# A vision-tower layer on one Trainium2 core: table stage, relu in PSUM and the last tree, changed together

## The reference

```python
dA = (1.0 + dtA / 2) / (1.0 - dtA / 2)
V = jnp.exp(log_dA[:, :, None] * jnp.arange(L))
K = 2.0 * jnp.einsum('chn,hnl->chl', C_term, V).real
```

```python
for level in range(DEPTH):
    n = 2 ** level
    g = gate[:, n - 1:2 * n - 1]
    f = jnp.stack([1.0 - g, g], axis=-1)
    lp = lp * broadcast(f).reshape(BT, M)
```

## Time and profile before

| what | value |
|---|---|
| times shown | 501.42, 502.08, 502.32 us |
| profiled execution, its own time | 502.32 us |
| its span, first to last instruction | 500.5 us |
| what lies around the span | 1.82 us |
| mean granted TensorE clock | 0.989 of full |
| busy: PE, DVE, ACT, POOL | 442.5, 353.1, 293.3, 193.0 us |
| chain that ended last, share by engine | PE 67%, DVE 14%, issue 6%, POOL 5%, ACT 3%, DMA 2% |

### The profile page before, as it was taken

How to read it: one execution, slowest core, us unless ns; L and a number is a source line. 1 busy time by engine, 2 the same in 40 slices (tenths; PEclk the granted TensorE clock), 3 DMA queues, 4 the chain that set the end, 5 groups by cost and what they waited for, 6 DMA issues and landing times.

```text
span 500.5 us, 11532 instructions
## 1 busy us (share of the span) xinstructions
PE 442.5 (88%) x3897; PEld 404.0 (81%) x3897; DVE 353.1 (71%) x837; ACT 293.3 (59%) x612; POOL 193.0 (39%) x185
## 2 busy tenths in 40 slices
PE   0099668899999999999999999999999999998993
PEld 0069667787888898988988988988988988988992
DVE  5999987997877785546486486486486486485685
ACT  3824654788876777467357357356356356356641
POOL 0495997642442110516306306306306306305102
PEclk9995999999999999999999999999999999999999
DMA  4541768444442211001002002002002001001002
GB/s 127 171 144 44 174 176 232 114 108 127 127 117 85 64 43 38 27 2 42 1 2 84 0 0 84 0 0 84 0 0 84 0 0 42 0 0 43 3 1 85
DMA packets 39904, 30.96 MB, mean 62 GB/s; under 512 B 19520, under 2 KB 35264, under 8 KB 39872
## 3 DMA queue, kind: packets, MB, share of 16 engines
q1 hardware_dynamic: 29024, 27.55, 18.4%
q10 hardware_dynamic: 10848, 3.02, 2.7%
HBM read 17.97 MB, written 12.58 MB: 61 GB/s over the span
## 4 chain that ended last, share of the span: by engine, by line
PE 67%; DVE 14%; issue 6%; POOL 5%; ACT 3%; DMA 2%; SPq 1%; POOLq 1%; DVEq 0%; ACTq 0%
PE PS L332 18%; PE PS L334 17%; PE PS L333 17%; PE PS L1625 5%; PE PS L1752 3%; PE PS L1667 3%; DVE XY L1033 2%; POOL Wb L511 2%; PE PS L1598 2%; DVE lTl L1317 1%; DVE outb L1377 1%; POOL Wa L511 1%; DMA craw<-in_c_ri 1%; DVE PS L1033 1%; PE PS L1634 1%
## 5 line engine op out<-in xcount | busy, mean ns | idle before, releaser
L1346 DVE TENSOR_TENSOR gl<-PS,gh 128x512 fp32r<-128x512 f32 x56 | 38.7, 691 | 62.1 <-ACT gh L851 34.5
L848 ACT ACTIVATE PS<-PS,fc1bias 128x512 f32<-128x512 f32 x56 | 36.7, 655 | 75.3 <-PE PS L334 74.4
L332 PE MATMUL PS<-fc2h,gh 128*128 128x256 f32 x256 | 73.6, 287 | 2.9 <-DVE gl L1346 1.5
L561 POOL TENSOR_SCALAR pst<-mv 128x4 f32<-128x4 f32 x15 | 4.2, 280 | 185.4 <-DVE pst L1330 185.4
L334 PE MATMUL PS<-fc2l,gh 128*128 128x256 f32 x256 | 71.5, 279 | 0.0
L333 PE MATMUL PS<-fc2h,gl 128*128 128x256 f32 x256 | 71.4, 279 | 0.0
L332 PE MATMUL PS<-x2Th,fc1h 128*128 (+2 forms) x144 | 54.5, 379 | 0.0
L332 PEld LDWEIGHTS PS<-fc2h,gh 128*128 128x128 f32 x256 | 48.0, 188 | 6.8 <-DVE pst L1330 1.6
L333 PE MATMUL PS<-x2Th,fc1l 128*128 (+2 forms) x144 | 53.0, 368 | 0.0
L334 PE MATMUL PS<-x2Tl,fc1h 128*128 (+2 forms) x144 | 52.9, 367 | 0.0
L333 PEld LDWEIGHTS PS<-fc2h,gl 128*128 128x128 f32 x256 | 48.2, 188 | 1.0
(11 more groups left out here) (254 smaller groups left out, 1442.7 us busy)
## 6 DMA issues: line engine op xcount, KB each, us to landing
h<-h_scratch SPq DMA_DIRECT2D x16, 256.0 KB, 3.7
q_scratch<-qe SPq DMA_DIRECT2D x16, 256.0 KB, 2.3
qf<-q_scratch SPq DMA_DIRECT2D x16, 256.0 KB, 2.9
out_tokens<-outb SPq DMA_DIRECT2D x14, 256.0 KB, 2.3
h_scratch<-tokev ACTq DMA_DIRECT2D x10, 256.0 KB, 2.9
craw<-in_c_ri SPq DMA_DIRECT2D x16, 128.0 KB, 2.6
craw<-in_c_ri SPq DMA_DIRECT2D x32, 64.0 KB, 2.4
h_scratch<-tokev SPq DMA_DIRECT2D x6, 256.0 KB, 2.8
```

Of the source, the lines that this page charges most:

```text
L332: pe.matmul(dst, ah, bh, start=start, stop=False, **kw)
L848: act.activation(bank(j % 2), bank(j % 2), ACT.Gelu, bias=fc1bias[:, j:j + 1]).then_inc(gact, 1)
L1346: dve.tensor_tensor(gl[:, j % 2, :], bank(j % 2), gh[:, j % 2, :].bitcast(F32), ALU.subtract).then_inc(gldone, 1)
```

## The change

1. SP: only the first half of iar is issued by SP, the other by ACT ahead of its two loads; the 768 KB of q, k, v weights are loaded right behind, ahead of btab and the constants.
2. ACT: `minus` and qkvh are made before the powers' squares; the copies of the third w, of the gate and of the leaf weights move ahead of the chunks; PE no longer waits for the powers before the six products of the low part, and its bias products lose one of three, which POOL adds later.
3. DVE: dA^192 by two scalar_tensor_tensor and two products in place of six operations; each doubling with four or five in place of six; the sum of chunk 0 before chunk 1's first product. ACT makes base[9] = 3 base[10] for it.
4. ACT: the stores of chunks 6 and 7 before the operands of 8 and 9.
5. relu of q and k in place in PSUM; DVE reads it there; PE waits for DVE (qdone, kdone) before it overwrites the bank. `k_elu` waits for ACT's third copy too.
6. Last group: tanh twice, with scale +s and -s, into alternating places, and one operation a level for both branches; POOL makes -s; the output bias goes to `att` without a wait for finish.

```diff
@@ SP
-            for rows in halves:
-                sp.dma_start(iar[rows, :], inv_ar).then_inc(ld_exp, 16)
+            sp.dma_start(iar[halves[0], :], inv_ar).then_inc(ld_exp, 16)
+            sp.dma_start(qkvraw[:, :, :], qkvT.rearrange("(k p) o -> p k o", p=P)).then_inc(ld_qkv, 16)
...
-            sp.dma_start(qkvraw[:, :, :], qkvT.rearrange("(k p) o -> p k o", p=P)).then_inc(ld_qkv, 16)
@@ POOL
+            scales(CHUNKS - FIRST + 2)
+            pool.wait_ge(b1copied, 1)
+            link(pool.tensor_tensor(fc1bias[:, :], b1raw[:, :], b1add[:, :], ALU.add))
...
+                pool.tensor_scalar(pst4[:, 3, x], pst4[:, 1, x], -1.0, None, ALU.mult).then_inc(zv4[h], 1)
...
-                pool.wait_ge(outdone, CREDIT + 2 * LAST)
-                pool.tensor_tensor(o1[:, x, :], h1[:, x, :], woutbias[:, :].unsqueeze(1).to_broadcast([P, 2, D]),
+                pool.wait_ge(x2T, CREDIT + GROUPS)
+                pool.tensor_tensor(att[:, x, :], h1[:, x, :], woutbias[:, :].unsqueeze(1).to_broadcast([P, 2, D]),
@@ ACT
+            act.dma_start(iar[N:P, :], inv_ar).then_inc(ld_exp, 16)
             for r in range(2):
                 act.dma_start(aim[r * N:(r + 1) * N, :], a_im).then_inc(ld_aim, 16)
...
             act.activation(Y[:, :, 0], btab[:, 1, :], ACT.Copy, scale=-2.0).then_inc(b_out, 1)
+            act.wait_ge(ld_const, 16 * 6)
+            act.activation(minus[:, :], ident, ACT.Copy, scale=-1.0).then_inc(minus_set, 1)
+            act.wait_ge(ld_qkv, 16)
+            act.activation(qkvh[:, :, :], qkvraw[:, :, :], ACT.Copy).then_inc(act_set, 1)
             act.wait_ge(dve_set, DVE_Z)
...
+            act.wait_ge(act_tab, 5 + 2 * (LOGS - 2))
+            act.activation(base[:, 9, :], base[:, 10, :], ACT.Copy, scale=3.0).then_inc(act_tab, 1)
...
+            act.wait_ge(qkvld, 3)
+            act.activation(bank(1), pwb[:, 2, :, :].rearrange("p x h -> p (x h)"), ACT.Copy).then_inc(pw_out, 1)
+            act.wait_ge(pe_set, 1)
+            act.activation(routraw[:, :, :].rearrange("p k x -> p (k x)"), bank(6), ACT.Copy).then_inc(gated, 1)
+            act.wait_ge(pe_set, 2)
+            act.activation(leafraw[:, :, :].rearrange("p k x -> p (k x)"), bank(5), ACT.Copy).then_inc(staged, 1)
...
-                act.activation(qr[:, :, :].rearrange("p o x -> p (o x)"), bank(5), ACT.Relu).then_inc(qact, 1)
+                act.activation(bank(5), bank(5), ACT.Relu).then_inc(qact, 1)
...
-                act.activation(kr[:, i, :], PS[:, b, 0:D], ACT.Relu).then_inc(kvact, 1)
+                act.activation(PS[:, b, 0:D], PS[:, b, 0:D], ACT.Relu).then_inc(kvact, 1)
...
-            next_opened(3, 0)
+            paired_tables(4, 1)
+            closed(3, 0)
+            paired_operands(4, 0)
+            m_unshifted(4, 0)
+            closed(3, 1)
             paired_operands(4, 1)
-            closed(3, 1)
...
-                    act.activation(th[:, 2 * h + t, :], last_rows(h, t), ACT.Tanh,
-                                   scale=pst4[:, 1, 2 * h + t:2 * h + t + 1]).then_inc(zth[h], 1)
+                    for s, sign in ((1, 1), (0, 3)):
+                        act.activation(last_signs(h)[:, t, :, s], last_rows(h, t), ACT.Tanh,
+                                       scale=pst4[:, sign, 2 * h + t:2 * h + t + 1]).then_inc(zth[h], 1)
@@ DVE
+            ur, ui1, ur2 = U[:, 0, 0, :], ui[:, 0, :], PS[:, 0, 0:H]
+            link(dve.scalar_tensor_tensor(PS[:, 3, 0:H], ur2, 4.0, base[:, 10, :], ALU.mult, ALU.subtract))
+            dve.wait_ge(act_tab, 7 + 2 * (LOGS - 2))
+            link(dve.scalar_tensor_tensor(PS[:, 2, 0:H], ur2, 4.0, base[:, 9, :], ALU.mult, ALU.subtract))
+            tt(ui[:, 2, :], PS[:, 3, 0:H], ui1, ALU.mult)
+            tt(U[:, 0, 2, :], PS[:, 2, 0:H], ur, ALU.mult)
...
+                if m < 4:
+                    t = t[:, 0:2 * H * m].rearrange("p (h x m) -> p h x m", x=2, m=m)
+                    tt(t, xy, wr, ALU.mult)
+                    tt(x_, y, wi, ALU.mult)
+                    link(dve.scalar_tensor_tensor(y_, x, -1.0, wi, ALU.mult, ALU.mult))
+                    tt(xy_, xy_, t, ALU.add)
+                else:
+                    t = t.rearrange("p (h m) -> p h m", m=m)
+                    tt(xy_, xy, wr, ALU.mult)
+                    tt(t, y, wi, ALU.mult)
+                    tt(x_, x_, t, ALU.add)
+                    tt(t, x, wi, ALU.mult)
+                    tt(y_, y_, t, ALU.subtract)
...
-            overlapped(0, 0)
+            product_sums(0, 0)
+            first_product(1, 1)
+            second_product(1, 1)
...
-                dve.scalar_tensor_tensor(q, q, 1.0, qr[:, :, :], ALU.min, ALU.add).then_inc(qdone, 1)
+                r = bank(5).rearrange("p (o x) -> p o x", o=KD)
+                dve.scalar_tensor_tensor(q, q, 1.0, r, ALU.min, ALU.add).then_inc(qdone, 1)
...
-                dve.wait_ge(kvact, CREDIT + 3 * n + 2)
+                dve.wait_ge(kvact, CREDIT + 3 * n + 3)
...
                 for level in range(max(first, 1), last):
                     n = 2 ** level
+                    pairs = dst[:, 0:4 * n].rearrange("p (m s) -> p m s", s=2)
+                    nodes = src[:, 0:2 * n].unsqueeze(2).to_broadcast([P, 2 * n, 2])
+                    dve.scalar_tensor_tensor(pairs, signs[:, :, n - 1:2 * n - 1, :], 1.0, nodes,
                                              ALU.add, ALU.mult).then_inc(done, 1)
-                    dve.scalar_tensor_tensor(pairs[:, :, :, 0], nodes, 2.0, pairs[:, :, :, 1],
-                                             ALU.mult, ALU.subtract).then_inc(done, 1)
@@ PE
-                pe.wait_ge(qact, CREDIT + 2 * s)
+                pe.wait_ge(qdone, CREDIT + s)
...
-                pe.wait_ge(kvact, CREDIT + 3 * (2 * s + i - 1))
+                pe.wait_ge(kdone, CREDIT + 2 * s + i - 1)
...
-            pe.wait_ge(dve_set, DVE_POWERS)
             pe.wait_ge(minus_set, 1)
...
-            pe.wait_ge(dve_set, DVE_POWERS + 12)
+            pe.wait_ge(dve_set, DVE_POWERS + 8)
...
-                pe.matmul(PS[:, 0, j:j + 1], ident, b1raw[:, j:j + 1], start=True, stop=False)
```

More of the change, by code:

```diff
@@ L543, in _ @@
                 scales(n - FIRST + 3)
-            for s in range(CHUNKS - FIRST + 2, STEPS):
+            scales(CHUNKS - FIRST + 2)
+            pool.wait_ge(b1copied, 1)
+            link(pool.tensor_tensor(fc1bias[:, :], b1raw[:, :], b1add[:, :], ALU.add))
+            for s in range(CHUNKS - FIRST + 3, STEPS):
                 scales(s)
@@ L649, in _ @@
                 act.activation(PS[:, 0, 0:H], power(j)[0], ACT.Square).then_inc(act_tab, 1)
+            act.wait_ge(act_tab, 5 + 2 * (LOGS - 2))
+            act.activation(base[:, 9, :], base[:, 10, :], ACT.Copy, scale=3.0).then_inc(act_tab, 1)
             act.wait_ge(dve_set, DVE_POWERS)
-            for j in range(3):
-                act.activation(bank((6, 7, 1)[j]), pwb[:, j, :, :].rearrange("p x h -> p (x h)"),
+            for j in range(2):
+                act.activation(bank((6, 7)[j]), pwb[:, j, :, :].rearrange("p x h -> p (x h)"),
                                ACT.Copy).then_inc(pw_out, 1)
@@ L659, in _ @@
                 if d == 2:
-                    act.wait_ge(dve_set, DVE_POWERS + 6)
+                    act.wait_ge(dve_set, DVE_POWERS + 4)
                 act.activation(U[:, 1, d, :], ui[:, d, :], ACT.Copy, scale=sgn[:, 0:1]).then_inc(u_out, 1)
-            act.wait_ge(ld_qkv, 16)
-            act.wait_ge(ld_const, 16 * 6)
-            act.activation(minus[:, :], ident, ACT.Copy, scale=-1.0).then_inc(minus_set, 1)
-            act.activation(qkvh[:, :, :], qkvraw[:, :, :], ACT.Copy).then_inc(act_set, 1)
             for c in range(3):
@@ L669, in _ @@
                 act.activation(qkvl[:, :, :].rearrange("p k x -> p (k x)")[:, c * 512:(c + 1) * 512],
-                               bank((4, 5, 0)[c]), ACT.Copy).then_inc(qkvld, 1)
+                               bank((4, 5, 1)[c]), ACT.Copy).then_inc(qkvld, 1)
+            act.wait_ge(qkvld, 3)
[4 more added lines that the diff above has]
+            act.activation(leafraw[:, :, :].rearrange("p k x -> p (k x)"), bank(5), ACT.Copy).then_inc(staged, 1)
             def operands(n):
@@ L773, in next_opened @@
                 m_unshifted(it + 1, par)
-            act.wait_ge(pe_set, 1)
-            act.activation(routraw[:, :, :].rearrange("p k x -> p (k x)"), bank(6), ACT.Copy).then_inc(gated, 1)
             opened(0, 0)
-            act.wait_ge(pe_set, 2)
-            act.activation(leafraw[:, :, :].rearrange("p k x -> p (k x)"), bank(5), ACT.Copy).then_inc(staged, 1)
             act.wait_ge(gated, 1)
@@ L782, in _ @@
             act.wait_ge(pe_set, 3)
-            act.activation(fc1bias[:, :], PS[:, 0, 0:JH], ACT.Copy).then_inc(b1copied, 1)
+            act.activation(b1add[:, :], PS[:, 0, 0:JH], ACT.Copy).then_inc(b1copied, 1)
             paired_tables(1, 0)
@@ L1069, in _ @@
             assert count[0] == DVE_POWERS, count[0]
-            t = PS[:, 2, 0:H]
```

(12 more changed lines are left out.)

57 lines of the change are left out of this document (28 added, 29 removed).

## The result

The changed kernel takes 499.29 us (median of four executions, 498.29 to 499.62); the kernel before, on the same chip, 502.20 (four executions, 501.42 to 502.34). The ratio is 0.9941, with a 95% interval of 0.9929 to 0.9954. The forecast was 494.9, the range 492.8 to 498.2. The profiled execution took 499.20, its span is 497.4 against 500.5. So 3.1 us were gained in the span and 2.9 in the median, where 7.4 were forecast.

What follows compares the result with a forecast made beforehand. Bounds were taken as DVE's table chain, POOL in the chunks from 48.17 until after 72 us, PE after 94, then DVE in the last group. Gains 4.7 + 1.3 + 1.4 = 7.4 from 502.32 gave 494.9, range 492.8 to 498.2.

Steps and rivals of the forecast that it cites:

- Start: Loads and ACT's work before the first square: square 0.2 us earlier, bounds 0.6 gained and 0.6 lost.
- POOL's cap: First chunks: POOL's own tables end at 43.45, so chunk 2 starts at most 4.73 us plus 0.2 earlier.
- Third power: DVE's table stage: four operations of 1.80 us replace six of 3.90; gain 2.1, bounds 1.6 and 2.2.
- Doublings: DVE's table stage, m = 1, 2, 4: fewer fixed costs; gain 1.0 us, bounds 0 and 1.8.
- Table copy and the sum's place: Before the first chunk: DVE's wait for the table copy shrinks by 0.5 us, moving sum M ahead gains 1.0.
- First chunk: Chunks' start: M ready 4.8 us earlier, POOL limits nearly the same; gain 4.7.
- PE's set-up: Rival: PE's gate weights and bias at the lower clock, chunk 0 starts at 42, not 39.3; 497.6 us, chance 0.1.
- Relu: First step: q_elu and k_elu undisturbed with a PSUM operand, PE starts earlier; gain 1.3 us, bounds 0 and 1.4.
- Last group: Tail: fewer tree operations, POOL's additions off the path, DVE's last pair earlier; gain 1.4 us, bounds 0.5 and 1.9.
- late start: Rival: constants or large load land 1.5 us later, squares start 1.3 late; 496.4 us, chance 0.15.

Runs made afterwards that it cites:

- copies_back: Changed kernel with the 768 KB load issued last on SP again and ACT's minus and qkvh behind the copies of the powers; 495.88 us.
- aim_first: Changed kernel with ACT issuing aim's two halves before iar's second half, the large load still early on SP; 499.91 us.
- load_after_btab: Changed kernel with SP issuing the 768 KB load behind the four loads of btab instead of in front; 498.03 us.
- before_early_load: Kernel before with only the changed order of loads, all copies left where they were; 504.43 us, ratio 1.0031 to 1.0055.
- before_relu: Kernel before with only relu of q and k written back to PSUM and read there by DVE, plus its waits; 501.01 us, ratio 0.9966 to 0.9983.
- all_mended: Changed kernel with large load last on SP, minus and qkvh later, POOL's additions behind each half's tree, 16 unused PE products; 495.05 us.
- after_filled: Changed kernel with only 16 unused PE products added between the transposes of the first leaf probabilities and the first leaf product; 497.88 us.

## Why the prediction was wrong, step by step

**Start: forecast 0.2 earlier, measured 2.2 later. This step failed.** The prediction looked for the delay at ACT's square ("if the constants or the large load land 1.5 us later") and gave the loss a bound of 0.6. The transfer that mattered was one whose own code the change does not touch, aim. In the kernel before, it had landed at about 4.6 us and was wanted at 6.15, so it had 1.5 us of slack; now it landed at 8.22, 3.6 later, of which 0.6 are its later issue and the rest its longer way. The 0.6 us that iar was to gain on ACT did not come either (copies_back). The Trainium skill, page "DMA: Bandwidth & Descriptors", section "Issuing engines are not separate DMA queues", was cited for the statement that the DMAs of all issuers interleave on the same 16 engines, and I drew from it only that iar's earlier issue gains nothing. The runs agree with the rule, and its consequence here was ten times as large: with the 768 KB load issued just ahead of it on the other engine, a 64 KB transfer took 6.25 and 6.5 us instead of 3.2 to 4.0 (changed kernel and aim_first, against aim's in the kernel before, load_after_btab, aim_first and copies_back). In the kernel before the delay went through whole (before_early_load: square 2.0 later, time 2.2 more); in the changed one POOL's cap hides some of it, and 1.5 are left at the first tanh (copies_back).

**Third power: forecast 2.1 saved, measured 3.90 - 1.85 = 2.05. Doublings: 1.0, measured 0.9**, with the wide operation of m = 1 at 1.10 us against the 1.05 that was put between its bounds. **Table copy and the sum's place: 0.5 and 1.0**, measured 0.49 and 0.78. Right, the last with 0.2 too much.

**First chunk: forecast 4.7, measured 2.3 at POOL.** With the start mended it is 3.76, so the start took 1.44 of the missing 2.4. The cap was the right mechanism, but mis-sized by 0.9: POOL's tables end at 43.85 in copies_back, 0.40 later than before (0.17 of it is the square), and between them and chunk 2 another 0.55 us of idling remain, which the prediction had counted as nothing. PE's set-up did not hold the chunk; its products ran at granted 0.50 from 28.19 to about 32, as the rival said, but then at 1.00 again. They ended at 37.5, and M came at 40.53.

**Relu: forecast 1.3, measured 1.25** in the median of before_relu and 1.45 in its profile, by the mechanism named. The Trainium skill, page "SBUF — State Buffer", section "Who interferes with whom", agrees with the runs in both places: DVE operations with two operands from SBUF took 1.33 and 1.72 us beside POOL here and 1.27 and 1.21 in the tail, and 0.68, 0.42, 0.18 and 0.19 with one operand in PSUM or with POOL out of the way. It explains the gain here, and it would have named the loss in the tail.

**Last group: forecast 1.4 gained, measured 1.46 lost. This step failed too,** not in the terms that it had but in two that it put at nothing: without these two disturbances it is 1.5 gained (14.03 to 12.52). The prediction said of POOL's additions that they "leave the path, since `att` is free long before", and put them "around 485". It asked only who waits for the addition, not what the addition would lie beside. Its new waits were all met when POOL's last rstd was done, at 480.69, and at that moment DVE was in the first tree, in operations with two operands from SBUF. The second disturbance, PE's clock at the end, appeared in neither the sum nor the rivals: a shorter tree does not only end earlier, it lets PE idle in other proportions (2.20 us idle ahead of 1.4 us of work, then 0.50). Both together cost 15.49 - 12.51 = 3.0 us in the profiled execution: 1.7 are POOL's, by the second tanh (6.40 against 4.68), and 1.3 the clock's, from there to the last pair (9.09 against 7.83). Both vary from profile to profile, POOL's share with a tenth of a microsecond in its start. (The 4.4 us that the prediction gives for the second tree before are 4.48 by its own rows; nothing hangs on it.)

**Sum.** At DVE's last pair 7.4 was forecast and 2.19 came: 1.44 lost by the start, 0.94 by the mis-sized cap, 2.86 by the last group (1.4 and 1.46). Behind the last pair 0.9 to 1.1 came back, since the last output transfers took 3.3 us in the profile of the kernel before and 1.8 in this one, for a reason that stays open; that makes the 3.1 of the span. all_mended, in which start and last group are repaired, gains 7.0 in its median and 6.5 at the last pair. Of the rivals only "late start" had the right place, with other transfers: it had the square 1.3 us later than before, measured 2.2. That its price, 1.5 us, is what the start did cost at the first tanh is luck, since the cap hid the rest; and its 496.4 was still 2.9 away. The range held neither the loss at the start (at most 0.6) nor one in the last group (at least 0.5 gained), so that both together fell outside it. Its low end was too low by its own cap on POOL: 4.73 + 0.6 for the chunks, with 1.4 and 1.9, makes 8.6 us, that is 493.7 and not 492.8.

## What to carry to other kernels

When a large load is moved forward, look first at the small transfers issued beside or just behind it by any engine, and at the slack of what waits for them, not at the load's own consumer. When an operation is freed to run earlier, find the moment at which its last wait is met, and read what the other engines do at that moment. When a serial stretch on DVE is shortened near the end, check where PE then idles, since its clock can take back what was gained.

## What the runs showed that I had not expected

- The granted clock in the tail does not follow from the gaps of the last group alone. before_relu has those of the kernel before, 0.88 us before the first transposes and 1.86 before the first leaf product, and yet the clock went to 0.50 at about 490 in its profiled execution, while it stayed at 1.00 in that of the kernel before:

```profile
488.00:490.00 2.00, 0.47 (x4) 0.23 (x3) 1.76 (x9) 0.60 (x1) 0.00 (x0) 0.93 0.00 0
490.00:492.00 2.00, 1.68 (x8) 1.71 (x9) 1.83 (x7) 0.00 (x0) 0.00 (x0) 0.50 0.00 0
```

It cost 15.15 - 14.03 = 1.1 us of tail in that execution. The twelve executions of before_relu have mean clocks from 0.979 to 0.992, so one profile shows one of several outcomes; what decides between them is open.
- A DVE operation of 16 elements that met a POOL addition of 2 x 1.26 us took 1.27 us instead of 0.18, the length of one of POOL's two instructions. One of 64 elements that met the second with half of it over took 0.68 instead of 0.21 (after_filled). The cost is set by what is left of the instruction that it meets, and not by its own size. The low part of x4 between them, with one operand in PSUM, took 0.74 us for its two operations beside the same addition and 0.76 without it.
